# An attention and MLP chain on one core: the rel tables spread by one instruction each, and the first image's loads, constant rows, rel transfers and bias products rearranged

## The reference

```
block 0 (12 heads of 16, windows of 14x14, image padded to 28x28):
    qkv  = window(layernorm(x)) @ qkv_w + qkv_b
    attn = (q * 16**-0.5) @ k.T + rel_h(q)[.., key row] + rel_w(q)[.., key column]
           rel_h = einsum('bhwc,hkc->bhwk', q, rel_pos_h[row - key row + 13])
    x   += (softmax(attn) @ v) @ proj_w + proj_b
    x   += gelu(layernorm(x) @ fc1_w + fc1_b) @ fc2_w + fc2_b
block 1 (12 heads of 48, one window of 16x16): the same form with its own weights
```

## Time and profile before

| | |
|---|---|
| median of 3 runs | 871.84 us (869.4 to 873.34) |
| profiled execution: time | 873.07 us |
| profiled execution: span | 871.2 us |
| TensorE (PE) busy | 768.9 us, 88% |
| VectorE (DVE) busy | 534.5 us, 61% |
| ScalarE (ACT) busy | 436.6 us, 50% |
| GpSimd (POOL) busy | 128.0 us, 15% |
| mean PEclk | 0.968 |

### The profile page before, as it was taken

How to read it: one execution, slowest core, us unless ns; L and a number is a source line. 1 busy time by engine, 2 the same in 40 slices (tenths; PEclk the granted TensorE clock), 3 DMA queues, 4 the chain that set the end, 5 groups by cost and what they waited for, 6 DMA issues and landing times.

```text
span 871.2 us, 18544 instructions
## 1 busy us (share of the span) xinstructions
PE 768.9 (88%) x6570; PEld 616.6 (71%) x6570; DVE 534.5 (61%) x1592; ACT 436.6 (50%) x1421; POOL 128.0 (15%) x243
## 2 busy tenths in 40 slices
PE   3679889898998977779979999999999999997998
PEld 2556657575675644678866887878787878766887
DVE  6156777757677677465425576756666666674552
ACT  2035565656556555444434555555556555554432
POOL 7200111101111010141330101010101010101111
PEclk9999999989999997799996999999999999999999
DMA  7312621010210100100040404040404040400001
GB/s 145 70 35 35 156 35 23 14 31 6 37 20 17 26 11 1 37 1 1 2 72 1 75 1 74 2 74 1 74 1 75 1 75 2 75 0 1 20 20 36
DMA packets 39147, 30.06 MB, mean 34 GB/s; under 512 B 12662, under 2 KB 37010, under 8 KB 39056
## 3 DMA queue, kind: packets, MB, share of 16 engines
q1 hardware_dynamic: 36030, 26.55, 16.2%
q0 software_dynamic: 2048, 1.89, 1.2%
q10 hardware_dynamic: 978, 0.43, 0.3%
HBM read 8.77 MB, written 1.57 MB: 12 GB/s over the span
## 4 chain that ended last, share of the span: by engine, by line
PE 71%; DVE 16%; issue 4%; ACT 3%; DMA 2%; POOL 2%; SPq 1%; ACTq 1%; DVEq 0%; POOLq 0%
PE bank L1270 10%; PE bank L526 7%; PE bank L1356 7%; PE bank L1297 5%; PE bank L1145 5%; PE bank L1277 4%; PE bank L976 4%; PE bank L952 4%; PE bank L1316 4%; PE bank L1077 3%; PE bank L1412 3%; DVE Pb L704 3%; DVE xhat L432 2%; PE bank L1003 2%; PE bank L506 2%
## 5 line engine op out<-in xcount | busy, mean ns | idle before, releaser
L693 ACT ACTIVATE Pb<-bank,nmax 128x256 f32<-128x256 f32 (+1 forms) x432 | 192.4, 453 | 90.0 <-DVE nmax L683 87.2
L683 DVE TENSOR_REDUCE nmax<-bank 128x2 f32<-128x392 f32 (+2 forms) x240 | 138.7, 579 | 45.7 <-PE bank L1270 34.0
L704 DVE TENSOR_SCALAR Pb<-Pb,rsum 128x196 f32<-128x196 f32 (+2 forms) x432 | 136.2, 353 | 8.5
L723 ACT COPY area<-bank 98x392 f32<-98x392 f32 (+1 forms) x144 | 77.5, 539 | 84.3 <-PE bank L1277 72.8
L1270 PE MATMUL bank<-QK 80*128 80x256 f32 x384 | 108.2, 407 | 10.6 <-DMA QK<-rel_dense 7.9
L1270 PEld LDWEIGHTS bank<-QK 80*128 80x128 f32 x384 | 69.2, 198 | 32.1 <-issue 16.5
L693 ACT ACTIVATION_READ_ACCUMULATOR Pb<-bank,nmax 128x1 f32 x432 | 87.4, 202 | 0.0
L976 PE MATMUL bank<-ident,Pb 128*98 128x128 f32 x384 | 63.4, 290 | 20.0 <-DVE Pb L704 19.9
L515 ACT ACTIVATE area<-bank,fc1b 128x256 f32<-128x256 f32 x96 | 45.2, 476 | 58.8 <-PE bank L506 51.3
L526 PE MATMUL bank<-fc2w,area 128*128 128x192 f32 x384 | 66.4, 332 | 0.0
L976 PEld LDWEIGHTS bank<-ident,Pb 128*98 128x98 f32 x384 | 41.2, 132 | 34.3 <-DVE Pb L704 29.1
(11 more groups left out here) (151 smaller groups left out, 1481.6 us busy)
## 6 DMA issues: line engine op xcount, KB each, us to landing
QK<-dense SPq DMA_DIRECT2D x32, 288.0 KB, 6.2
QK<-dense SPq DMA_DIRECT2D x48, 64.0 KB, 2.4
QK<-dense SPq DMA_DIRECT2D x90, 28.0 KB
QK<-rel_dense SPq DMA_DIRECT2D x32, 48.0 KB, 3.3
QK<-rel_dense POOLq DMA_DIRECT2D x32, 48.0 KB, 3.0
out<-x_all SPq DMA_DIRECT2D x8, 192.0 KB, 2.0
x_all<-in_x SPq DMA_DIRECT2D x1, 1344.0 KB, 16.6
QK<-in_c_hot SPq DMA_DIRECT2D x2, 384.0 KB, 5.1
```

What stands on the lines that cost most here:

```text
L683: nc.vector.tensor_reduce(nmax[0:sc.shape[0], u % 3, 0:sc.shape[1]], sc, AX.X, ALU.max, negate=True).then_inc(self.m_rdy, 1)
L693: nc.scalar.activation(Pb[u % 3][0:rows, t, 0:cols], sc[:, t, :], ACT.Exp, bias=nmax[0:rows, u % 3, t:t + 1], accum_out=esum[0:rows, u % 3 ...
L704: nc.vector.tensor_scalar(Pb[u % 3][0:rows, t, 0:keep], Pb[u % 3][0:rows, t, 0:keep], rsum[0:rows, u % 3, t:t + 1], None, ALU.mult).then_i ...
L723: copy(*self.pt_views(u)).then_inc(self.pt[self.pt_engine(u)], 1)
```

## The change

1. `spread` writes a whole table with one instruction of 14 x 84 = 1176 columns (block 1: 16 x 32 = 512) from an access pattern with overlapping windows. Lines lie in reverse order, and the matmuls read them so. Both tables of block 0 are now made by VectorE, one after the other; GpSimd makes none.
2. The constant rows of K for `K0[0]` go from VectorE to GpSimd, ahead of the `c_hotpad` transfers; GpSimd's memsets of V no longer wait for xhat. ScalarE loads Q's rows before K's, copies the first half of Q's constants ahead of its xn and the second half behind it, and issues the tables of block 1 behind the first q group and the bias loads behind the second one.
3. SP issues `late` directly behind `first`, then image 1 alone. Images 2 to 7 are loaded behind the rel transfers of the first image.
4. Of the 12 rel transfers of image 0, SP issues the six of the h table as soon as that table is evicted and two of the w table later. ScalarE issues four.
5. kpad scaling and vb spreading move ahead of the first image's v on VectorE. The table products of block 1 move in front of v on TensorE. The bias products come behind the first scores and ahead of the third unit's scores, and VectorE adds them to `obias` ahead of the third maximum; TensorE waits for that addition behind its three scores.
6. VectorE's wait for the norm vectors moves from ahead of the statistics to behind xhat.

```
-        rest = [(flip[:], a["c_flip31"]), (blk1[:], a["c_blk1"])]
-        rest += table_loads(2, "L1_conv_rel_pos_0") + table_loads(3, "L1_conv_rel_pos_1")
-        rest += [(obias[0][:], bcast(a["L0_conv_proj_b"])), (obias[1][:], bcast(a["L1_conv_bo"]))]
+        tables_rest = [(flip[:], a["c_flip31"]), (blk1[:], a["c_blk1"])]
+        tables_rest += table_loads(2, "L1_conv_rel_pos_0") + table_loads(3, "L1_conv_rel_pos_1")
+        obias_rest = [(obias[0][:], bcast(a["L0_conv_proj_b"])), (obias[1][:], bcast(a["L1_conv_bo"]))]
...
-        operand_rows = [(k_const[D0:K0ROWS, :], a["c_hot0"]), *at_remainder(k_const, a["c_hotrem"], 2 * WS),
-                        *at_remainder(q_const, a["c_qwin"], 0)]
+        key_rows = [(k_const[D0:K0ROWS, :], a["c_hot0"]), *at_remainder(k_const, a["c_hotrem"], 2 * WS)]
+        query_rows = list(at_remainder(q_const, a["c_qwin"], 0))
...
-                if meanwhile:
+                if meanwhile and which == "act":
                     meanwhile(eng)
                 if which == "pe":
                     for u in range(3):
+                        if meanwhile and u == 2:
+                            meanwhile(eng)
                         self.pe_scores(eng, Img(0, 0), u)
                 elif which == "act":
                     for u in range(2):
                         self.act_exp(eng, Img(0, 0), u)
                 else:
                     for u in range(3):
+                        if meanwhile and u == 2:
+                            meanwhile(eng)
                         self.dve_max(eng, Img(0, 0), u)
                     self.dve_norm(eng, Img(0, 0), 0)
+
+                if before_values:
+                    before_values(eng)
...
-                    eng.wait_ge(relw_h0_done, WS)
-                    eng.wait_ge(relw_w0_done, WS)
+                    eng.wait_ge(relw_h0_done, 1)
+                    eng.wait_ge(relw_w0_done, 1)
...
+                    if n.index0():
+                        self.scatter_rel(eng, p, range(GH0), (0,))
                     eng.wait_ge(self.g_out[0], n.at(6, 4))
                     land(eng, "sp")
-                    self.scatter_rel(eng, p, range(GH0 // 2) if n.index0() else range(GH0))
+                    if n.index0():
+                        self.scatter_rel(eng, p, range(2, GH0, 2), (1,))
+                    else:
+                        self.scatter_rel(eng, p, range(GH0))
...
+        a0 = Attention0(0, lambda n: ({0: ld_x0, 1: ld_x1}.get(2 * n.pair + n.par, ld_x), 16), xdone[0], L0_UNITS, {6 * q + 5: [q] for q in range(3)})
...
             win, heads, blk = relw_spec[i]
-            for line in range(win):
-                row = reltab[i][:, win - 1 - line:2 * win - 1 - line]
-                yield engine.tensor_tensor(relw[i][:, line, :, :], row.unsqueeze(1).broadcast_to([CH, heads, win]),
-                                           blk[:].unsqueeze(2).broadcast_to([CH, heads, win]), ALU.mult)
+            windows = bass.AP(reltab[i], 0, [[2 * win - 1, CH], [1, win], [0, heads], [1, win]])
+            blocks = blk[:].unsqueeze(1).unsqueeze(3).broadcast_to([CH, win, heads, win])
+            return engine.tensor_tensor(relw[i][:, :, :, :], windows, blocks, ALU.mult)
...
-            pe.wait_ge(ld_w, 16 * len(rest))
-            table_products(1)
             pe.wait_ge(prep_dve, 4)
-            pe.wait_ge(prep_dve, 6)
+            pe.wait_ge(tables1_done, 2)
...
-            pe.wait_ge(obias_done, 2)
...
+        def dve_values(dve):
+
+            dve.wait_ge(ld_first, 16 * len(first))
+            for at in (0, HALF):
+                nc.vector.tensor_scalar(KP0[at:at + D0], kpad0[at:at + D0].unsqueeze(2).broadcast_to([D0, NPAIR, N0]),
+                                        D0 ** -0.5, None, ALU.mult).then_inc(kpad_done, 1)
             dve.wait_ge(ld_zeroed, 16 * len(late))
             for l, (v, k) in enumerate(((vb0, 3), (vb1, NPAIR))):
                 nc.vector.tensor_copy(vbc[l], v[:].unsqueeze(2).broadcast_to([P, k, P])).then_inc(prep_dve, 1)
-            for at in (0, HALF):
-                nc.vector.tensor_scalar(KP0[at:at + D0], kpad0[at:at + D0].unsqueeze(2).broadcast_to([D0, NPAIR, N0]),
-                                        D0 ** -0.5, None, ALU.mult).then_inc(kpad_done, 1)
+            dve.wait_ge(prep_pe, 4)
+            for i in (2, 3):
+                nc.vector.tensor_copy(reltab[i][:], tab_bank[0:CH, 32 * i:32 * i + 31]).then_inc(tables1_done, 1)
+
+        def dve_meanwhile(dve):
             dve.wait_ge(prep_pe, 6)
-            dve.wait_ge(ld_w, 16 * len(rest))
+            dve.wait_ge(ld_obias, 32)
...
-            sp.dma_start(x_all[:, NT:, :], x_view[:, NT:, :]).then_inc(ld_x, 16)
             sp.wait_ge(zeroed, len(zero_weights))
-            sp.wait_ge(zeroed_even, 4)
             for dst, src in late:
                 sp.dma_start(dst, src).then_inc(ld_zeroed, 16)
+            sp.dma_start(x_all[:, NT:2 * NT, :], x_view[:, NT:2 * NT, :]).then_inc(ld_x1, 16)
+            sp.wait_ge(zeroed_even, 2)
+            sp.wait_ge(zeroed_even_k, 2)
+
             def load_later():
-                sp.wait_ge(zeroed_odd, 4)
+                sp.dma_start(x_all[:, 2 * NT:, :], x_view[:, 2 * NT:, :]).then_inc(ld_x, 16)
                 for dst, src in later:
                     sp.dma_start(dst, src).then_inc(ld_later, 16)
+                sp.wait_ge(zeroed_odd, 4)
...
+                pool.wait_ge(ld_rows0, 16 * len(key_rows))
+                constant_rows(pool, nc.gpsimd.tensor_copy, k_const, K0[0], zeroed_even_k, 1)
                 pool.wait_ge(zeroed_pad, 3)
                 for dst, src in first_rows:
                     pool.dma_start(dst, src).then_inc(ld_const, 16)
-                pool.wait_ge(a0.norm.xhat, NT)
                 for z in zero_v:
                     nc.gpsimd.memset(z[:], 0.0).then_inc(zeroed_v, 1)
                 pool.wait_ge(zeroed_v, 4)
-                pool.wait_ge(ld_rows0, 16 * len(operand_rows))
+                pool.wait_ge(ld_qrows0, 16 * len(query_rows))
                 constant_rows(pool, nc.gpsimd.tensor_copy, k_const, K0[1], zeroed_odd, 1)
                 constant_rows(pool, nc.gpsimd.tensor_copy, q_const, Q0[1], zeroed_odd, 3)
-                pool.wait_ge(prep_dve, 2)
-                for instruction in spread(nc.gpsimd, 1):
-                    instruction.then_inc(relw_w0_done, 1)
...
+            def tables1(pe):
+                pe.wait_ge(ld_w, 16 * len(tables_rest))
+                table_products(1)
+
+            def obias_read(pe):
+                pe.wait_ge(obias_done, 2)
+            a0.run(pe, "pe", pe_meanwhile, {2: tables, 7: tables1}, before_values=obias_read, following=lambda e, part: m0.start(e, "pe", a0, part))
...
-            for dst, src in operand_rows:
+            for dst, src in query_rows:
+                act.dma_start(dst, src).then_inc(ld_qrows0, 16)
+            for dst, src in key_rows:
                 act.dma_start(dst, src).then_inc(ld_rows0, 16)
-            for dst, src in rest:
-                act.dma_start(dst, src).then_inc(ld_w, 16)
-            act.wait_ge(ld_rows0, 16 * len(operand_rows))
-            constant_rows(act, nc.scalar.copy, q_const, Q0[0], zeroed_even, 0)
+
+            def constant_queries(half):
+                nc.scalar.copy(Q0[0][HALF * half:HALF * (half + 1)],
+                               q_const[:].unsqueeze(1).broadcast_to([HALF, NPAIR, T])).then_inc(zeroed_even, 1)
+            act.wait_ge(ld_qrows0, 16 * len(query_rows))
+            constant_queries(0)
             act.wait_ge(ld_norm, 16 * len(for_norm))
 
             def loaded(act):
+                constant_queries(1)
                 act.wait_ge(ld_first, 16 * len(first))
+
+            def load_tables(act):
+                for dst, src in tables_rest:
+                    act.dma_start(dst, src).then_inc(ld_w, 16)
+
+            def load_obias(act):
+                for dst, src in obias_rest:
+                    act.dma_start(dst, src).then_inc(ld_obias, 16)
 
             def scatter_first(act):
                 act.wait_ge(a0.g_out[0], 4)
                 act.wait_ge(a0.g_out[1], 4)
-                a0.scatter_rel(act, 0, range(GH0 // 2, GH0))
+                a0.scatter_rel(act, 0, (0, 1, 3, 5), (1,))
                 act.wait_ge(zeroed_v, 4)
 
             def start_mlp0(act, part):
                 act.wait_ge(ld_later, 16 * len(later))
                 act.wait_ge(ld_chunked, 16 * len(chunked))
                 m0.start(act, "act", a0, part)
-            a0.run(act, "act", between={2: loaded, 7: scatter_first}, following=start_mlp0)
+            a0.run(act, "act", between={2: loaded, 3: load_tables, 4: load_obias, 7: scatter_first}, following=start_mlp0)
...
-            dve.wait_ge(ld_norm, 16 * len(for_norm))
+
+            def scale_loaded(dve):
+                dve.wait_ge(ld_norm, 16 * len(for_norm))
 
             def tables(dve):
 
@@ -1753,14 +1793,11 @@
                 for i in (0, 1):
```

(32 more changed lines are left out.)

11 lines of the change are left out of this document (5 added, 6 removed).

## The result

The changed kernel takes 860.58 us (median of 4 runs, 859.17 to 863.09) beside 870.66 us for the kernel before (4 runs). The ratio is 0.9883, interval 0.9846 to 0.992: 10.1 us less, 1.2%. The forecast was 862.0, in a range from 855.5 to 867. The number came out; the way to it did not, as the profile shows.

A forecast was written before the change was run, and what follows sets the result against it. The prediction took the serial chain of waits up to the first transposed probabilities at 53.07 us as the bound. Terms -5.7, -1.8 and -2.4 gave -9.9, so 871.84 became 862.0 us, range 855.5 to 867.

The forecast's parts named there:

- Up to the rel products: Front of image 0: rel products start at 19.7 instead of 25.41 us, -5.7, from an earlier start and a closed gap.
- The spread: VectorE in the front: one 1176-column instruction takes 1.39 us, two take 2.8, done at about 14.7.
- The 3.2 us for the closed gap: TensorE's q and k matmuls: 3.2 of the 5.7 us gained, by no longer standing still ahead of the second k group.
- rival A: TensorE's clock rises early, at the start of the rel products: they take 4.4 instead of 8.04 us; total 856.5; chance 0.2.
- the prediction's own sign (28 records under 3 us): Rel products of image 0: 28 L1145 records under 3 us would mean an early clock rise and a wrong prediction.
- The rel transfers: ScalarE ahead of v's eviction: four issues take 3.6 us instead of six in 5.38, -1.8.
- ScalarE's six later loads are issued behind q evictions, while it waits for TensorE: nothing: Front, ScalarE's queue: issuing block 1's tables and the biases later was claimed to cost no time.
- would cost up to 0.9: Block 1's table products on TensorE: hidden beside ScalarE's transfers with 0.3 us to spare; uncovered, up to 0.9 us.
- The tail: From first scores to first transposed probabilities: 9.2 us, against 11.60 before from the remainder of v's end, -2.4.
- B: Part of the front's cover fails: slow spreads give 867.7, a late landing of `first` or hotpad 864; chance 0.2.
- C: First units after the bias products run at the lower clock: gain lost or slower, up to 890; chance 0.05.
- D: Front shortens as forecast, but image 2 or MLP 0 waits for loads: at most the gain is lost, 872; chance 0.03.

## Why the prediction was right, and where its steps were not

**The number.** 862.0 against 860.58, or -9.9 against -10.1. That they agree so well is luck, as the terms below show. In the profiled executions the front gained 11.3 (forecast 9.9), and the rest of the span another 2.5. The latter is no part of the argument: behind the first transposes the spans of the 14 profiles are 813.0 to 819.4 us long, with no order by edit.

**Up to the rel products: right in kind, short in size.** `first` did become last, and landed at 8.64, at the early end of 8.7 to 12.4; I had taken the middle, 1.9 us too late. q and k ran without a gap, as forecast, but in 6.0 us instead of 7.4. The rel products started at 16.16, not 19.7: -9.3 instead of -5.7.

**The spread: right in size, wrong in worth.** 1.39 us forecast, 1.37 measured. The 3.2 us for the closed gap were a term of the sum; in the changed kernel the tables' landing hides them (the run with 28 instructions), and in the kernel before GpSimd's table does.

**The rel products: rival A.** 4.49 us instead of 8.02. I had called the lower level the likelier, at 0.52 to 0.2. Over the nine profiles with the new front they took 4.49, 4.49, 4.49, 6.00, 6.09, 6.09, 6.33, 6.41 and 7.53 us, and 8.02 with the spread by lines; in the kernel before and its three variants, 7.93 to 8.02. So neither case is right as a fixed value. In all nine the q and k products took less than the 7.4 us of the kernel before (5.9 to 7.05), so the level rose within them; what differs is when it fell again. In six profiles the granted clock fell within the rel products, with TensorE at work, and in the three with 4.49 us it fell 0.3 to 0.5 us behind their end. By the prediction's own sign (28 records under 3 us) its mechanism was wrong here.

**The rel transfers: right.** 3.62 us forecast as 3.6; by itself the split brought the forecast 1.8 us up to the remainder of v, and 0.7 more through a higher level in the bias products.

**The step that failed: "ScalarE's six later loads are issued behind q evictions, while it waits for TensorE: nothing".** I priced what these transfers cost the engine that issues them, and wrote of the table products that without cover they "would cost up to 0.9". I did not price when they land. Their consumer had moved forward too, from the end of the front to ahead of v. They took 16.05 us where I had small columns at 2.2 to 5.9; and the hotpad transfers, moved by the same change from 6.6 to 11.0, made them late. The trace of before held the warning: hotpad itself took until 25.9 from 6.64. The stop is 8.0 us in this profile and 5.8 in the second one of the same kernel, whose rel products took longer; both end with the landing, at 28.7 and 28.8.

**How the errors cancelled.** By the forecast's times the rel products end at 27.7, and the first scores start 43.2 - 9.2 = 34.0. Measured: 20.65 and 33.73. What the early landing of `first` and the upper level gave, 7.0 us, the stop took, 6.8. The two are not independent: TensorE could not start the tables before they landed at 28.65, however early it was. Luck is that this landing fell within 1 us of 27.7, where the forecast had the rel products end. The tail took 8.04 us instead of 9.2, since the bias products ran partly at the upper level (4.50 instead of 5.41).

**The rivals.** A came true for the rel products of this profile, but not for v and the scores: the lower level was back there, at full price, with the stop and without it. B had the right form, a cover that fails, but not this one. A and B both named a late hotpad landing, for GpSimd's gather (28.57 here, 30.0 in A); that it makes other transfers late was in neither. C did not come: the bias products raised the level as before, and scores behind them took 0.93 us. D named loads as the danger, but those of image 2; no wait on them appears.

**The rule on the shared port.** The Trainium skill (SBUF — State Buffer, section "SBUF: two separate sides") says that, of a VectorE instruction with two SBUF inputs and a GpSimd instruction that reads SBUF, the one that starts first keeps the shared port and the other waits for its whole length. The runs agree in both directions: GpSimd's copies grew by 1.06 us beside a spread that was there first, and with hotpad ahead a spread that met a K copy took 2.63 us instead of 1.37. In that run xhat, too, took 1.94 us instead of 0.67 while GpSimd issued hotpad, most of which was hidden under the landing of `first`: the table products started at 8.61, but the q and k products waited 0.2 us for xnT. The slow spreads left a gap of 0.45 us ahead of the second k group.

## What to carry to other kernels

When a transfer is moved, price its landing against its consumer, not only its issue; and when a slow transfer moves later, ask which small ones now travel beside it. When TensorE runs slowly behind a stop, look at where the granted clock fell before giving the stop the blame: here it fell in six profiles within the rel products, and taking the stop away did not bring the faster level back. A wait for a landing absorbs whatever was gained ahead of it. A sum that fits the total proves no term of it: here two errors of 7 us each cancelled, and only the chain of waits told.

## What was not expected of the hardware

- Four small transfers of tables (31 rows, 11.6 KB for each of the two larger) on ScalarE's queue had landed 16 us after the last was issued while two transfers of 142 KB from GpSimd's queue were under way, and after at most 12 with those issued 5.4 us earlier.
- The changed kernel's 56 rel records took 4.49 us in one profile and 6.33 in another: the granted clock fell 0.4 us behind them in the one, and in their midst in the other, without a pause of TensorE. With extra matmuls of 128x128 behind them it rose again in the midst of these, 3.2 us after their start in one run and 5.9 in another.
- PEclk reads 1.00 for the q and k products of the changed kernel, although they run slower than the same form later (16 records in 6.04 us against 8 in 1.89); the column shows the lower level only from the first fall on, and in the run with the spread by lines it reads 1.00 for the whole front, with rel products of 8.02 us.
